# Two zero-writes and their waits put ahead of each pair of table look-ups on GpSimd, in a recommendation kernel on one Trainium2 core

## What is computed

```
p = emb[:, ROW];  q = emb[:, COL]                  # 496 pairs of 32 fields
kp = einsum('bpj,ipj->bpi', p, kernel)             # kernel: 64 x 496 x 64
z = sum(kp * q, axis=-1)                           # 1024 x 496
h = concatenate([z, dense_ctx], axis=1)            # + 16 dense columns
h = relu(h @ W_top1 + b_top1)                      # 512 wide
h = relu(h @ W_top2 + b_top2)                      # 256 wide
y = h @ W_top3                                     # 1024 x 1
```

## Time and profile before

| What | Value |
|---|---|
| Median of 3 runs | 498.26 us (494.0 to 500.97) |
| Span of the profiled execution, first to last instruction | 412.5 us |
| PE busy | 403.7 us (98%) |
| DVE busy | 298.6 us (72%) |
| ACT busy | 259.1 us (63%) |
| POOL busy | 231.6 us (56%), 251 instructions |
| Mean granted TensorE clock | 0.996 |

### The profile page before, as it was taken

One profiled execution on the slowest core, in us unless ns is written; L12 is line 12 of the kernel. 1 busy time (PEld: TensorE's weight loads), 2 busy tenths in 40 slices (PEclk: granted clock), 3 DMA queues, 4 the chain that ended last, 5 costly groups with the idle time before them and its releaser, 6 DMA issues.

```text
span 412.5 us, 10180 instructions
## 1 busy us (share of the span) xinstructions
PE 403.7 (98%) x3421; PEld 254.4 (62%) x3421; DVE 298.6 (72%) x293; ACT 259.1 (63%) x1874; POOL 231.6 (56%) x251
## 2 busy tenths in 40 slices
PE   7889999999999999999999999999999999999997
PEld 5556656667675766666766665666666566654442
DVE  6776887878788887878979798878879888740000
ACT  6476877667577876764796867719978667002221
POOL 6777777777677757776766777677767200000000
PEclk9998999999999999999999999999999999999999
DMA  6665661131281111211211113111311020000000
GB/s 177 210 200 155 191 221 33 27 77 27 37 219 28 29 19 47 61 28 25 63 42 28 25 25 79 24 27 26 79 25 27 15 51 2 2 2 0 2 0 1
DMA packets 18266, 24.31 MB, mean 59 GB/s; under 512 B 6387, under 2 KB 11767, under 8 KB 17958
## 3 DMA queue, kind: packets, MB, share of 16 engines
q1 hardware_dynamic: 10406, 15.64, 13.0%
q0 software_dynamic: 7808, 8.01, 9.7%
HBM read 19.44 MB, written 0.00 MB: 47 GB/s over the span
## 4 chain that ended last, share of the span: by engine, by line
PE 92%; DMA 3%; POOL 3%; issue 1%; ACT 0%
PE u_ps L690 41%; PE z_ps L724 14%; PE u_ps L711 13%; PE z_ps L730 7%; PE u_ps L771 7%; PE t_ps L644 4%; PE u_ps L791 3%; POOL nat L419 3%; DMA nat<-tbl,ids_sb 2%; PE u_ps L697 2%; DMA ids_sb<-ids 1%; PE t_ps L677 0%; PE u_ps L799 0%; ACT y_sb L571 0%
## 5 line engine op out<-in xcount | busy, mean ns | idle before, releaser
L419 POOL DMA_INDIRECT nat<-tbl,ids_sb x244 | 230.5, 945 | 90.7 <-issue 56.6
L607 DVE TENSOR_TENSOR prod<-u_ps,rows 128x1024 f32<-128x1024 f32 x184 | 213.5, 1218 | 56.7 <-PE u_ps L690 56.7
L504 ACT ACTIVATE pass_prod<-pass_prod 128x64 f32<-128x64 f32 x896 | 214.3, 243 | 22.1 <-DVE pass_prod L618 22.1
L690 PE MATMUL u_ps<-rows,k_sb 64*128 64x256 f32 x1472 | 176.2, 387 | 0.0
L504 ACT ACTIVATION_READ_ACCUMULATOR pass_prod<-pass_prod 128x1 f32 x896 | 169.9, 190 | 0.0
L690 PEld LDWEIGHTS u_ps<-rows,k_sb 64*128 64x128 f32 x1472 | 139.0, 188 | 46.0 <-DVE pass_prod L618 13.4
L618 DVE TENSOR_TENSOR pass_prod<-u_ps,nat 128x1024 f32<-128x1024 f32 x56 | 67.2, 1215 | 1.2 <-PE u_ps L711 1.2
L711 PE MATMUL u_ps<-k_sb,rows 64*128 64x256 f32 x448 | 61.5, 394 | 0.6 <-ACT rows L492 0.6
L724 PE MATMUL z_ps<-prod,sel 128*32 128x512 f32 x512 | 61.6, 598 | 0.0
L492 ACT ACTIVATE rows<-t_ps 128x512 f32<-128x512 f32 (+1 forms) x38 | 19.6, 516 | 54.2 <-PE t_ps L644 54.0
L711 PEld LDWEIGHTS u_ps<-k_sb,rows 64*128 64x128 f32 x448 | 40.6, 186 | 14.6 <-DVE prod L607 9.6
(11 more groups left out here) (50 smaller groups left out, 78.9 us busy)
## 6 DMA issues: line engine op xcount, KB each, us to landing
by_self<-rows SPq DMA_DIRECT2D x32, 128.0 KB
nat<-tbl,ids_sb POOLq DMA_INDIRECT x244
k_sb<-kern SPq DMA_DIRECT2D x3, 768.0 KB, 5.6
k_sb<-kern SPq DMA_DIRECT2D x2, 640.0 KB, 5.7
k_sb<-kern SPq DMA_DIRECT2D x1, 1152.0 KB, 5.2
k_sb<-kern SPq DMA_DIRECT2D x2, 512.0 KB
rows<-w SPq DMA_DIRECT2D x1, 1024.0 KB, 6.6
rows<-tbl SPq DMA_DIRECT2D x4, 224.0 KB
```

What stands on the lines that cost most here:

```text
L419: pool.indirect_dma_start(nat_of(m, n)[:, h * EMBED:(h + 1) * EMBED], None, tables[f], bass.IndirectOffsetOnAxis(ids_sb[:, col:col + 1], 0 ...
L504: op = nc.scalar.activation(of, of, ACT.Copy, accum_out=z_nat[:, b % 2, s, row:row + 1])
L607: nc.vector.tensor_tensor(to, u, by.unsqueeze(1).to_broadcast([P, 2, 2, SIZE]), ALU.mult).then_inc(prod_ready, 1)
L690: op = nc.tensor.matmul(u[:, h, :], k_sb[part, k_of(d), side, :], rows[part, tile, cols_of(b)], start=True, stop=True)
```

## The change

From tile 12 on, in each of the two sub-blocks, GpSimd writes zeros to a new buffer `zeros` (128 partitions of 128 floats, read by nobody), waits until this is done, does both again, and then issues the sub-block's two gathers. 52 tiles with 2 sub-blocks give 104 such places and 208 memsets.

```diff
 AHEAD = 30
+SPACED = 12
...
         sel = sb("sel", [P, 62])
+        zeros = sb("zeros", [P, P])
...
+        zeros_there = sem("zeros_there")
...
                         if quads:
                             pool.wait_ge(summed, quads)
+                        if m >= SPACED and h == 0:
+                            for turn in range(2):
+                                nc.gpsimd.memset(zeros[:], 0.0).then_inc(zeros_there, 1)
+                                pool.wait_ge(zeros_there, 4 * (m - SPACED) + 2 * n + turn + 1)
                         f = 2 * tile + h
```

## The result

| | Before | With the change |
|---|---|---|
| Median of 4 runs each | 497.08 us (494.0 to 500.97) | 502.32 us (501.65 to 506.02) |
| Profiled span | 412.5 us | 499.9 us (that execution took 501.65) |

The ratio is 1.013, 95% interval 1.0084 to 1.0176: slower by 5 to 6 us, and the same by the measure of 2%. The forecast was 540 us. Ratios, intervals and differences leave out slow runs (over 1.5% above the fastest of their kernel), which are two of the four of the changed kernel run again (median 503.95 us) and two of the seven of the kernel before in a later set (median 497.93 us, 493.5 without them).

What follows compares the result with a forecast made beforehand. TensorE bounds the kernel, with GpSimd nearly full; 96 places at 0.60 us (57.6) less 16.1 us of slack add 41.5 to the 412.5 us span, 454.0, plus 85.8 outside it: 539.8 us, range 512 to 584.

Steps and rivals of the forecast that it cites:

- the sum against the shown trace: Whole program: profiled span 412.5 plus 41.5 us of lateness, plus 85.8 us by which timed runs exceed it, about 540 us.
- the slack: At tile 59, TensorE wants the tile at 305.30 and GpSimd could have it there at 289.2: 16.1 us.
- the prediction's own formula: Lateness of tile 59: 96 places times x, less the slack of 16.1 us; 41.5 us at x = 0.60.
- taken x of 0.60: Two memsets with their waits lengthen GpSimd's way from one gather to the next by 0.60 us.
- What bounds the kernel: PE, busy for 403.7 of 412.5 us, with POOL nearly full too, occupied about 95% until its last gather.
- The period of 1.248 us: On POOL before the change, gathers start 1.248 us apart, from the 2nd to the 37th.
- the landing of some 1.4: A gather's data lands some 1.4 us after GpSimd has issued it.
- The low bound: x = 0.46 us on GpSimd: two turns of 0.20 plus 0.18, replacing 0.30 us idle, with no gap before the first memset.
- The roles change, and TensorE waits at its transposes: POOL sets the pace at 6.19 us a tile against TensorE's 5.25; pair 58/59 is the last wait, 41.5 us late.
- the memsets hide: Rival: the memsets run in POOL's 0.30 us idle time ahead of gathers; price 0 to 10 us, 498 to 508; 12%.
- If POOL never waited: From tile 12 on POOL's waits for PE vanish, so tile 59's last gather could start at 286.9 instead of 300.80.
- The clock at nothing: TensorE's clock falls at waits, 1.7 us more work a pair, covered by 1.9 us idle: priced at nothing.

Runs made afterwards that it cites:

- the 413 level: Kernel before, unchanged, in three of the five sets of runs: 412.94, 413.12 and 413.02 us; the trace shown ahead of the prediction is of this level.
- the 495 level: Kernel before, unchanged, in the other two of the five sets of runs: 495.16 and 497.93 us; the runs timed with the prediction are of this level.
- one turn: The change with one memset and one wait in each place instead of two: 422.18 us, ratio 1.0218 to the kernel before.
- the third set: The changed kernel, unaltered, run once more in a further set beside the kernel before: 500.33 us, ratio 1.0125.
- six cases: The change at both kernel-before times (413, 495 us); one turn and one ahead of each gather (413); five and ten turns (495): ratios 1.0218 to 1.3699.
- the gathers are unpaced: Kernel before, but from tile 12 on no gather waits for pieces or quads: 412.8 us (ratio 0.9993) in one set, 645.97 us (1.307) in another.
- without the gathers: Kernel before with the gathers of tiles 32 to 63 left out: 412.76 us (ratio 0.9998) in one set, 454.67 us (0.9219) in another.

## Why the prediction was wrong

**The step that failed** is the sum against the shown trace: "a span of 412.5 + 41.5 = 454.0, and with the 85.8 us by which the median of the runs lies above the profiled span, 539.8 us". The 85.8 us don't lie outside the span. In the profiled execution with the change 501.65 - 499.9 = 1.8 us do, and in the kernel before 494.78 - 493.0 = 1.8. The 85.8 are inside the program: TensorE is slower at the level at which the runs were timed. And with that the slack, which decides everything, was mis-sized: 16.1 us in the shown trace, 75.8 at the timed level. With 75.8 the prediction's own formula gives 96 x 0.46 - 75.8, below zero, even at its taken x of 0.60 (57.6 us): no change.

Point by point:

- *What bounds the kernel*: TensorE, right at both levels. "TensorE takes the tiles at 5.25 us each" holds at the 413 level only. From pair 18/19 to pair 58/59 the kernel before takes 381.40 - 121.18 = 260.2 us at the 495 level, 6.5 us a tile. GpSimd with the change needs 4 x 1.248 + 2 x 0.46 = 5.9 us, more than 5.25 and less than 6.5. This is the whole verdict.
- *The period of 1.248 us and the landing of some 1.4*: right (1.25; 1.5 to 1.6).
- *x = 0.60*: measured 0.463. The low bound was the right one, and right in that there is no gap ahead of the first memset. That it is met to the hundredth is luck: it took 0.58 us up to the second memset's end and 0.18 from there to the gather, where 0.48 to 0.49 and 0.27 were measured, and both make 0.76. The taken value rested on the single turn at the start (0.45 from start to start), where a second turn now costs 0.27 (x of 0.463 against 0.194 for one), and the first, 0.22 for the memset and 0.27 to the gather in place of the usual 0.30, adds 0.19. The Trainium skill, "Perfetto Trace Analysis", section "GPSIMD Engine Instruction", prefers spacing to spans. Spacing was the right thing to measure, but I took it from one place whose waiting instruction was of another kind.
- *The roles change, and TensorE waits at its transposes*: not at the timed level, where the rival "the memsets hide" (12%) has the right result by luck, since x was not small but the slack large. At the 413 level it is shown, with the first wait at pair 18/19 and the last at 58/59 as predicted. The predicted span was 454.0, measured 446.4; with the right x the prediction's sum would be 440.9.
- *"If POOL never waited"*: the waits for PE don't all vanish; 2.8 us remain at the 413 level, 5.2 with one turn.
- *The clock at nothing*: nearly right at the 413 level. It did fall while the waits lasted (mean 0.95 from 95 to 337 us), and the 2009 matmuls of that stretch kept TensorE busy for 219.4 us, where it was 210.0 for 2010 of them between 95 and 305 us in the trace shown before. The waits paid for these 9.4 us, as the prediction reckoned. Behind the last wait the clock was 0.50 for 3.4 us and TensorE fell back by another 2.7 us (33.9 in the span, 31.2 at pair 58/59); the single fall was priced at 1.7. The row:

```profile
338.00:341.40 3.40, 3.40 (x18) 0.68 (x12) 0.00 (x0) 3.40 (x28) 2.71 (x6) 0.50 0.11 19
```

- *Chances*: 87% for slower rested on one trace. That the trace and the runs differed by 85.8 us should have opened a rival, "the runs are of slower executions than the trace, with a larger slack", ending at no change. I explained the gap instead of asking what it was.

**Still open.** The 5 us by which the change is slower at the 495 level (1.013, 1.0092 and 1.0125 in three sets) are not late gathers: the shortest distance between a gather's end and its transposes is 2.49 us in the first of these traces and 1.66 in that of the third set, and landing is 1.5. The last gather starts 4.7 us later than in the kernel before (408.36 against 403.66). That the memsets change how densely the gathers lie, and by that how long TensorE is held, I had thought; VectorE's late starts speak against it (80 and 79 us in two traces with the change, 85 before). The difference goes with the granted clock: span times mean clock is 478.4 us over 16 executions of the kernel before and 479.0 over 10 of the changed one, while the spans are 493.6 and 499.6 us and the mean clocks 0.969 and 0.959. An estimate, since idle time has no clock; and what lowers the clock isn't shown. Open too is what separates the levels.

## What to carry to other kernels

Compare the profiled span with the timed runs before using either: a gap of 17% with nothing to fill it meant here that the trace was of another level, and the slack read from it wasn't the slack of the runs. An edit on an engine off the critical path costs (added time) - (slack), with the slack taken as wanted time minus earliest possible time over the whole stretch; this held within 6 us in six cases at both levels. If GpSimd gathers stand beside dense TensorE work, keep them paced, because back-to-back runs cost nothing on one level and 30% on the other.

## What the runs showed of the hardware that was not expected

- The same program takes 413 or 495 us, steadily within a set of runs. At the 495 level TensorE is held back while GpSimd's indirect DMAs are issued and for 1 to 2 us behind them; mostly it shows as products that VectorE starts up to 3 us (8 to 9, once 21, when the gathers are unpaced) after TensorE's rows for their piece end. The effect grows with density: 39 us for 128 paced gathers, 152 us more when those from tile 12 on are issued in runs, back to back. VectorE's products, two inputs each, keep their length: 1218 ns in the shown trace and 1219 at the 495 level.
- The Trainium skill, "Trainium Architecture — The Big Picture", section "What this means for kernel authors", says that SBUF's engine side and its DMA side can't contend, and that within the engine side only the ports shared by VectorE and GpSimd do. If it is so, the hold-up lies elsewhere; the runs don't show where. The same section calls the engines independent unless a semaphore ties them; at the 413 level the runs agree (0.9998 without the gathers), at the 495 level they don't (0.9219).
- A memset of 128x128 floats on GpSimd takes 0.21 us (208 in 44.0 us); a second turn with its wait adds 0.27 us from gather to gather, and the first, which takes the place of the usual 0.30 us, adds 0.19.
